# Cross-attention on one core: absorbed queries split by batch instead of by row group, first context turned earlier, first loads reordered

## The reference

```python
x = x + _L0_xattn_ref(_layernorm(x, axis=-1), ctx_768, Wq, Wk, Wv, Wo, bo)
...
q = hidden_states @ Wq
k = encoder_hidden_states @ Wk
v = encoder_hidden_states @ Wv
scores = jnp.einsum('bhsd,bhkd->bhsk', q, k) * scale
probs = jax.nn.softmax(scores, axis=-1)
out = jnp.einsum('bhsk,bhkd->bhsd', probs, v)
out = out.transpose(0, 2, 1, 3).reshape(B, S, H * Dh)
out = out @ Wo + bo
```

## Time and profile before

| what | value |
|---|---|
| median of three runs | 1573.8 us (1572.8 to 1575.11) |
| the profiled execution, its own time | 1573.21 us |
| span of its trace | 1571.4 us |
| PE busy | 1511.5 us, 96% |
| DVE, ACT, POOL busy | 1121.0, 731.6, 385.6 us |
| granted TensorE clock, mean | 0.989 |
| projections, 0 to 188.45 us | 188.45 us |
| first tile, to the second tile's first score | 56.42 us |
| second tile, to the third's | 53.53 us |
| one tile of the loop | 49.75 us |

### The profile page before, as it was taken

One profiled execution on the slowest core, in us unless ns is written; L12 is line 12 of the kernel. 1 busy time (PEld: TensorE's weight loads), 2 busy tenths in 40 slices (PEclk: granted clock), 3 DMA queues, 4 the chain that ended last, 5 costly groups with the idle time before them and its releaser, 6 DMA issues.

```text
span 1571.4 us, 35367 instructions
## 1 busy us (share of the span) xinstructions
PE 1511.5 (96%) x13421; PEld 1259.9 (80%) x13421; DVE 1121.0 (71%) x2240; ACT 731.6 (47%) x1532; POOL 385.6 (25%) x225
## 2 busy tenths in 40 slices
PE   7999877999999999999999999999999999998989
PEld 6888777888888988889988898878878878786544
DVE  7666758877778777787778877656555564556788
ACT  5444635555455554555455554433223232224755
POOL 1000233444444454444544444400000000000000
PEclk9999979999999999999999999999999999999999
DMA  7899795446554555545654464250310311323022
GB/s 241 317 368 362 289 307 155 109 145 172 166 170 98 161 169 169 165 102 171 169 169 142 115 180 145 89 194 22 110 67 29 124 40 42 108 82 129 2 106 107
DMA packets 148590, 235.90 MB, mean 150 GB/s; under 512 B 75345, under 2 KB 101393, under 8 KB 145681
## 3 DMA queue, kind: packets, MB, share of 16 engines
q1 hardware_dynamic: 148496, 234.57, 46.5%
HBM read 165.59 MB, written 68.94 MB: 149 GB/s over the span
## 4 chain that ended last, share of the span: by engine, by line
PE 85%; issue 7%; DVE 4%; DMA 3%; ACT 1%; SPq 0%; POOLq 0%; POOL 0%; DVEq 0%; ACTq 0%
PE psum_o L670 16%; PE psum_q L647 8%; PE psum_s L647 8%; PE psum_o L1482 6%; PE psum_q L1522 6%; PE psum_q L698 6%; PE psum_q L1482 6%; PE psum_t L1554 6%; PE psum_o L562 5%; PE psum_o L685 5%; PE psum_t L658 3%; DMA c_blk<-in_ctx_dram 2%; PE psum_s L1509 1%; PE psum_t L594 1%; PE psum_q L594 1%
## 5 line engine op out<-in xcount | busy, mean ns | idle before, releaser
L670 PE MATMUL psum_o<-pT,c_nat 128*128 128x512 f32 x1152 | 283.9, 397 | 27.1 <-issue 14.7
L670 PEld LDWEIGHTS psum_o<-pT,c_nat 128*128 128x128 f32 x1152 | 212.8, 189 | 76.7 <-issue 16.6
L1272 POOL TENSOR_TENSOR c_nat<-c_raw,constants 128x768 fp32r<-128x768 f32 x64 | 109.1, 1704 | 500.1 <-PE psum_o L670 386.7
L861 ACT ACTIVATE probs<-psum_s,nmax 128x257 f32<-128x257 f32 x128 | 61.1, 477 | 297.9 <-DVE nmax L1150 297.9
L647 PE MATMUL psum_s<-cT_high,qk 128*128 128x258 f32 x768 | 167.6, 294 | 0.1
L647 PE MATMUL psum_q<-cT_high,qk 128*128 128x258 f32 x768 | 153.8, 286 | 2.5 <-DVE qk L1063 2.5
L1136 DVE TENSOR_SCALAR oT<-psum_o,c_last 128x512 f32<-128x512 f32 x192 | 139.2, 745 | 21.9 <-PE psum_o L670 21.9
L928 DVE TENSOR_TENSOR pT<-psum_t,pT 128x512 fp32r<-128x512 f32 x128 | 87.7, 686 | 77.3 <-ACT pT L742 77.3
L1257 POOL TENSOR_TENSOR c_raw<-c_raw,last_row 128x768 f32<-128x768 f32 x64 | 118.0, 1843 | 65.4 <-DMA last_row<-in_ctx_dram 50.0
L647 PEld LDWEIGHTS psum_s<-cT_high,qk 128*128 128x128 f32 x768 | 130.1, 193 | 3.9 <-DVE cT_low L1113 0.6
L647 PEld LDWEIGHTS psum_q<-cT_high,qk 128*128 128x128 f32 x768 | 124.2, 189 | 5.6 <-DVE qk L1063 2.9
(11 more groups left out here) (299 smaller groups left out, 3364.8 us busy)
## 6 DMA issues: line engine op xcount, KB each, us to landing
qk_by_tile<-staged SPq DMA_DIRECT2D x32, 1536.0 KB, 10.4
raw<-qk_by_tile SPq DMA_DIRECT2D x16, 3072.0 KB, 13.9
c_raw<-in_ctx_dram SPq DMA_DIRECT2D x64, 384.0 KB, 3.5
c_blk<-in_ctx_dram SPq DMA_DIRECT2D x256, 96.0 KB, 2.4
last_row<-in_ctx_dram SPq DMA_DIRECT2D x64, 192.0 KB, 5.1
x_res<-in_x_dram SPq DMA_DIRECT2D x16, 256.0 KB, 2.6
out_dram<-x_res SPq DMA_DIRECT2D x16, 256.0 KB, 2.0
x_in<-out_dram SPq DMA_DIRECT2D x4, 1024.0 KB, 7.3
```

The source lines that it names most:

```text
L670: i = pe.matmul(ps[:], c_nat[(b - 1) % 2][:, part, k, m * P:(m + 1) * P], pT[:, moving, k, :], start=(k, part, moving) == (0, 0, 0), stop= ...
L1272: G.tensor_tensor(flat(c_nat[i][:, 0, :, :]), flat(c_raw[i][:]), zero.to_broadcast([P, 2 * DC]), ALU.add).then_inc(s_chi, 1)
```

## The change

- The parts of a tile's absorbed queries are slices by batch (`qk_of`, `raw_of`): slice `b` holds all heads of batch `b`, again 128x1536 elements. `pe_scores` waits for slice `b` at the first row group of each batch, and no longer for one part at each row group of batch 0.
- In the loop and in the last tile, slices 0 and 1 of the next tile are made at the end of b = 3, on DVE behind the second piece of `oT`; slices 2 and 3 are made within their own tile: on ACT at the end of b = 0, on DVE in b = 1 between the turn and the two low parts of the value product. The first and second tile have their own places.
- As `raw` comes free later, SP's wait and the load of the next tile's `raw` move from b = 0 to b = 1 (they stay in b = 0 in the second tile). In the last tile the first loads of the self-attention move with them.
- At the end of the projections the turn of the first context, its high part and its low part go in among the last query products; the high parts of slices 0 and 1 stand behind j = 4 and 6; POOL makes the low parts of slices 0 and 1.
- SP loads the blocks of batches 1 to 3 and the `raw` of the second tile ahead of the wait for the staged stores, then `wv`, the bias and the residual, and `wo_raw` after the blocks of batches 4 and 5.
- In batch 1 of the first tile `pe_probsT` stands behind S(1,1).

The diff, cut:

```diff
 def pe_scores(pe, t, b, rg, section):
             if rg == 0:
                 pe.wait_ge(s_ctlo, 4 * t + (b + 1))
-            if b == 0:
-                pe.wait_ge(s_qlo, 4 * t + (rg + 1))
+                pe.wait_ge(s_qlo, 4 * t + (b + 1))
...
+        def raw_of(b):
+            return raw[:].rearrange("p h r (c b q) -> p b (r c) h q", c=KC, b=4)[:, b]
+
+        def qk_of(part, b):
+            return qk[:, part].rearrange("p r c b (h q) -> p b (r c) h q", h=4)[:, b]
+
+        def act_qk_high(act, t, b):
...
+            nc.scalar.activation(qk_of(0, b), raw_of(b), ACT.Copy).then_inc(s_qhi, 1)
...
 def act_project_all(act):
+                    if (s, j) == (GROUPS - 1, 4):
+                        act_last_column(act, 0, 0)
+                    if (s, j) == (GROUPS - 1, 5):
+                        act_context_high(act, 0, 0)
...
 def act_cross_tile(act, t, section):
                 if b == 3 and more:
+                    if begun:
+                        act_qk_high(act, t + 1, 0)
                     act_qk_high(act, t + 1, 1)
                 act_last_scalars(act, t, b, section)
+                if b == 0:
+                    if section != "second":
+                        act_qk_high(act, t, 2)
+                    act_qk_high(act, t, 3)
...
-                if b == 3 and more:
-                    act_qk_high(act, t + 1, 2)
-                    act_qk_high(act, t + 1, 3)
...
 def dve_cross_tile(dve, t, section):
             if not begun:
                 dve_turn(dve, 4 * t, 1)
                 row_max(0, 0)
-                dve.wait_ge(s_qlo, 2)
-                dve_qk_low(dve, 0, 2)
                 row_max(0, 1)
-                dve_qk_low(dve, 0, 3)
...
                 norm(0, 3)
+                dve.wait_ge(s_qlo, 2)
+                dve_qk_low(dve, t, 2)
...
                 if after:
                     dve_turn(dve, 4 * t, b + 1)
+                if (section, b) == ("first", 1):
+                    dve_qk_low(dve, t, 3)
+                if (section, b) == ("first", 3):
+                    dve_qk_low(dve, t + 1, 0)
+                if (section, b) == ("second", 0):
+                    dve_qk_low(dve, t, 2)
+                if b == 1 and section not in ("first", "second"):
+                    dve_qk_low(dve, t, 2)
+                    dve_qk_low(dve, t, 3)
...
-                if qk_next:
-                    dve_qk_low(dve, t + 1, 0, section)
                 dve_attended(dve, t, b, 0, section)
...
                 dve_attended(dve, t, b, 1, section)
-                if qk_next:
-                    dve_qk_low(dve, t + 1, 2, section)
-                    dve_qk_low(dve, t + 1, 3, section)
+                if b == 3 and more:
+                    if begun:
+                        dve_qk_low(dve, t + 1, 0)
+                    dve_qk_low(dve, t + 1, 1)
+                if (section, b) == ("second", 0):
+                    dve_qk_low(dve, t, 3)
...
 def sp_cross_tile(sp, t, section):
-                if b == 0:
+                if b == (0 if section == "second" else 1):
                     sp.wait_ge(s_qlo, 4 * t + 4)
```

More of the change, by code:

```diff
@@ L705, in pe_cross_tile @@
                 before = begun or b > 0
+                late = not begun and b == 1
                 pe_scores(pe, t, b, 0, section)
-                if before:
+                if before and not late:
                     pe_probsT(pe, t, b, section)
                 pe_scores(pe, t, b, 1, section)
+                if late:
+                    pe_probsT(pe, t, b, section)
                 pe_scores(pe, t, b, 2, section)
@@ L1055, in dve_start_weights, with dve_qk_low @@
                 project_low(dve, ("WK", r, c), part[1], part[0], lambda ps: ps[:].rearrange("p (j n) -> p j n", j=4))
-        def dve_qk_low(dve, t, rg, section=None):
-            if section:
-                full(dve, U1(("S", 3, rg), t - 1, section))
-            dve.wait_ge(s_qhi, 4 * t + (rg + 1))
-            part = [qk[:, i, rg, :, :, :].rearrange("p c b (h q) -> p h (c b) q", h=4) for i in range(2)]
-            nc.vector.tensor_tensor(part[1], raw[:, :, rg, :].rearrange("p h (a q) -> p h a q", q=SQ), part[0].bitcast(F32),
-                                    ALU.subtract).then_inc(s_qlo, 1)
+        def dve_qk_low(dve, t, b):
+            dve.wait_ge(s_qhi, 4 * t + (b + 1))
+            nc.vector.tensor_tensor(qk_of(1, b), raw_of(b), qk_of(0, b).bitcast(F32), ALU.subtract).then_inc(s_qlo, 1)
         def dve_project_all(dve):
@@ L1203, in dve_cross_tile @@
                     inverse(b, 2)
-                if qk_next:
-                    dve_qk_low(dve, t + 1, 0, section)
                 dve_attended(dve, t, b, 0, section)
                 inverse(b, 3)
-                if qk_next and not begun:
-                    dve_context_low(dve, 4 * t, b + 1)
-                    dve_qk_low(dve, t + 1, 1, section)
-                    norm(b, 2)
-                    norm(b, 3)
-                    dve_attended(dve, t, b, 1, section)
-                    dve_qk_low(dve, t + 1, 2, section)
-                    dve_qk_low(dve, t + 1, 3, section)
-                    dve_attended(dve, t, b, 2, section)
-                    continue
-                if qk_next:
-                    dve_qk_low(dve, t + 1, 1, section)
                 if after:
@@ L1282, in pool_bias, with pool_qk_low @@
             nc.gpsimd.tensor_tensor(x_res[:], x_res[:], bo_all[:], ALU.add).then_inc(s_xb, 1)
-        def pool_qk_low(pool, t, rg):
-            pool.wait_ge(s_qhi, 4 * t + (rg + 1))
-            part = [qk[:, i, rg, :, :, :].rearrange("p c b (h q) -> p h (c b) q", h=4) for i in range(2)]
-            nc.gpsimd.tensor_tensor(part[1], raw[:, :, rg, :].rearrange("p h (a q) -> p h a q", q=SQ),
-                                    part[0].bitcast(F32), ALU.subtract).then_inc(s_qlo, 1)
+        def pool_qk_low(pool, t, b):
+            pool.wait_ge(s_qhi, 4 * t + (b + 1))
+            nc.gpsimd.tensor_tensor(qk_of(1, b), raw_of(b), qk_of(0, b).bitcast(F32), ALU.subtract).then_inc(s_qlo, 1)
         def pool_first_tile(pool):
@@ L1295, in pool_first_tile @@
             pool_split(pool, 0, 0, "first")
-            for rg in range(2):
-                pool_qk_low(pool, 0, rg)
-            pool.wait_ge(s_qlo, 4)
+            for b in range(2):
+                pool_qk_low(pool, 0, b)
+            pool.wait_ge(s_ctlo, 2)
             pool_split(pool, 0, 1, "first")
@@ L1306, in pool_cross_tile @@
             for b in range(4):
-                if section == "second" and b == 0:
-                    pool.wait_ge(s_qlo, 4 * t + 4)
-                    pool_less_last(pool, t, b + 1)
-                    pool_split(pool, t, b, section)
-                    continue
                 pool_split(pool, t, b, section)
@@ L1399, in sp_project_all @@
                         load_x_group(sp, s + 2)
-            for i in range(4):
-                sp.wait_ge(s_staged[i], 32 * GROUPS)
             load_blocks(sp, 0, 2)
@@ L1404, in sp_project_all @@
             load_ctx(sp, 0, 3)
+            load_blocks(sp, 0, 3)
+            sp.wait_ge(s_qlo, 4)
             load_qk(sp, 0, 1)
-            load_blocks(sp, 0, 3)
-            sp.wait_ge(s_nat, 3)
-            load_ctx(sp, 0, 4)
-            sp.dma_start(wo_raw[:], Wo.rearrange("(k p) n -> p k n", p=P)).then_inc(s_wo, 16)
+            for i in range(4):
+                sp.wait_ge(s_staged[i], 32 * GROUPS)
             sp.dma_start(wv[:], Wv.rearrange("(k p) n -> p k n", p=P)).then_inc(s_wvo, 16)
```

45 lines of the change are left out of this document (19 added, 26 removed).

## The result

The changed kernel takes 1546.8 us (median of 4 runs, 1545.59 to 1548.05) against 1573.3 before in the same series of runs, 0.9831 of it (95% interval 0.9814 to 0.9848). The profiled execution took 1546.91 us with a span of 1545.1.

What follows compares the result with a forecast made beforehand. PE was taken to bound the kernel, with at most 0.82 us a tile to win in the loop and 14.5 us of idle PE in the first tile. 1573.2 - 9.5 (start) - 8.4 (loop, last tile) gave 1555 us; range 1547 to 1567.

Steps and rivals of the forecast that it cites:

- End of the projections: Last query products ahead of the first tile: moving the first context's turn, high and low part there wins 1.7 us.
- Loads of the first tile: Start: the fifth batch's blocks land near 227.5, not 238.18; -9.5 us, the 1.7 of the projections included.
- The second tile: Second tile: one late low part fewer, two more in b = 0, later wo_raw; set to 0, with 2.5 us either way.
- Loop and last tile: Wait in b = 0 goes (-0.81), b = 1 loses 0.2: -0.6 us a tile, -8.4 in all.
- The last tile: Last tile: first self-attention rows load 9.5 us later; at most 1.4 us lost, once, taken as 0.
- rival 1: Loop: DVE and POOL meet in b = 1, the new loss equals the old 0.81; 1564 us, chance 0.20.
- rival 2: First tile: loads only change places, the fifth blocks land as late as at 238; 1563 us, chance 0.12.
- rival 4: b = 1: the first low part waits 3.1 us for POOL, 1.9 us lost a tile; 1590 us, chance 0.06.
- rival 5: Whole kernel: no change to speak of, rival 1 and rival 2 together; 1571.5 us, chance 0.06.
- Rival 3: Start and loop: no load binds in the first tile, the 0.81 goes whole; -16.2 - 11.3, 1546 us, chance 0.08.

Runs made afterwards that it cites:

- the repeated run: The change with the loop's slices made at the end of b = 3 again, high part ahead of exp(3,1), raw loaded in b = 0: 1561.55 us.
- the run with two more edits: The change with last-tile statistics all taken in b = 2, and the second tile's slices 2 and 3 and low parts of wo moved: 1546.2 us.

## Why the prediction was wrong

**End of the projections:** right in kind; 2.2 us instead of 1.7.

**Loads of the first tile:** right in mechanism, sized a little low. The blocks of the fifth batch were put at 227.5 and land at 224.74: `raw` was issued at 204.72, not 205.9, and the 6.23 MB from there on had landed after 20.0 us, not after 18.9 + 2.7. The second tile starts 6.3 us behind the landing, where 6.7 were taken. With the second tile the start gave 11.7, not 9.5. The second tile itself, set to 0, lost 2.1 of the first tile's gain (13.8 to 11.7).

**Loop and last tile:** the step that failed is a term of the sum, "Net -0.81 + 0.2 = -0.6 a tile", with its bound of 0.81. A tile gained 1.25. The 0.65 that are missing, times 13, are 8.4, about the whole miss of 8.2. That the two agree so well is luck: the start gave 2.2 more than its term, and the last tile 2.3 less (1.7 lost where 0.6 was to be gained). Three parts were mis-sized, all readable in starts of products, which are not modelled as ends are (medians of the 13 tiles):

- The wait ahead of PV (probabilities times context) in b = 0 costs 1.08, not 0.81. From the last score's start to the first PV product's start are 1.10 us before and 0.12 with the change, 0.98; the first PV product then takes 0.33 to the next instead of 0.23, another 0.10.
- The output product waited too, for ACT. From the last PV product's start to its own are 0.31 us before, 0.23 after, and 0.34 instead of 0.23 to the next product: 0.19 together. The waits view of PE does not list it, but that of the weight loads (PEld) of the kernel before does (below), 4.5 us in 13 waits for `probs`. With the change no weight load of the output product waits; with all slices in their old places (the repeated run) it is again 4.5 us in 13 waits, and with the high part alone behind exp(3,2) 12.4. I had asked of ACT only whether it had time for the high parts, not what stood behind them.
- b = 1 costs 0.04, not 0.2: the first PV product is followed after 0.28 instead of 0.24. That the first low part would wait about 0.5 us for POOL's bias, and no more, was right.

Together these are 1.23 of the 1.25. Two rows of the changed kernel show the first point, the last score and the first PV product in b = 0:

```profile
339.99 0.28 PE L646 MATMUL psum_q<-cT_high,qk 128*128 128x258 f32 x1
340.10 1.09 PE L669 MATMUL psum_o<-pT,c_nat 128*128 128x512 f32 x4
```

The waits of the weight loads in the kernel before (total us, times, longest) show the first point, nearly 1 us a time, and the second with its cause:

```profile
PEld psum_o L670 <- issue: 16.6, 17, 1.4
PEld psum_q L698 <- ACT probs L861: 4.5, 13, 0.4
```

The sentence that the loop "can give at most 0.82 us a tile" was the root: it took span less busy time for PE's idle time, and the busy time of the kernel before held 0.41 us of waiting. The Trainium skill says at the head of its page "Perfetto Trace Analysis" that matmul busy time is a bad measure, because matmuls are pipelined, and points to the busy share of the weight loads. The trace agrees: in the windows of one tile PE's idle time falls by 0.82 us, from 0.82 to nothing, but the idle time of the weight loads by 1.27, from 49.75 - 44.08 = 5.67 to 48.52 - 44.12 = 4.40, which is the gain.

**The last tile:** priced at up to 1.4 us and taken as 0, as PE was said to be ahead there. It was not: DVE waited 1.75 us, PE then 2.03 at 948.49, and from 949.5 to 952.5 the granted clock was at 0.50, the lower of its two levels (1.2 GHz). The tile lost 1.7 against the kernel before, and with the statistics moved it takes 49.91 instead of 52.44.

**Rivals.** A tile of 48.5 us and blocks that land at 224.74 rule out rivals 1, 2, 4 and 5 for the change; how near the loss in b = 1 was, the run with one more POOL operation shows. Rival 3, "more is won", names nearly the measured time (1546), but by luck: it has no load bind in the first tile, and there DVE still waits 1.73 us for one, while the loop gives more than the 0.81 that it takes as the most.

## What to carry to other kernels

Do not bound a gain by span less busy time: products overlap (here scores start 0.12 us apart and are listed with 0.28 each), so measure a tile from start to start, look at each product's distance to the next, and read the waits of the weight loads beside those of the products. When an operation is moved off an engine's queue, ask for every bank and buffer that the instructions behind it release, not only for the one wait that the view lists. An engine at 25% can still set the pace if it stands beside another one's work in the one place without room.

## What the runs showed of the hardware

- DVE's and POOL's operations with two inputs in SBUF wait for each other in both directions: a low part and a bias side by side took 4.76 (for two) and 2.67 us, against 3.42 and 1.27 where they did not have to wait.
- In the run with two more edits, a wait of 2.28 us on PE was followed by products at a third more time (5.97 instead of 4.38 us for 18). The granted clock was 1.00 to the end of the wait and 0.50, the lower of its two levels, from 268 to 270 us, so this wait cost more than its own length. Not each wait of about that length does: behind the one of 1.96 us at 258.01 in the changed kernel the clock stayed at 1.00.
- A small load right behind which a large one is issued lands later: `last_row` took 5.1 us with `raw` issued 0.6 us behind it and 3.3 alone; over twelve tiles of the loop the median is 5.6. In the changed kernel, where `raw` follows it after 1.3 us, the median is 3.6. With `raw` gone from b = 0, POOL's wait for it was gone.
